# A transformer layer in fp32 on one NeuronCore: PSUM banks of the 16-head attention from one pool of seven by a table, its order and the order of local attention anew

## The chip, the cores and the metric

The kernel runs on one core of one Trainium2 chip. The metric is the device time of one execution in microseconds (us), lower is better. Engines: PE (TensorE, with PEld for its weight loads), DVE (VectorE), ACT (ScalarE), POOL (GpSimd) and SP, which only issues DMAs. Each engine executes its own instruction stream in order; they meet through semaphores.

## What is computed

Eight batches of 512 tokens with 256 channels go through one post-norm layer: self attention with 16 heads of 16 channels, cross attention of the same form against a context of 512 tokens per batch, and then a stack of two layers of local attention (8 heads of 64, windows of 128 keys and the window before) with a gated MLP, seen as 8 x 512 tokens. Everything is fp32; products that need fp32 accuracy are made from two halves of each operand (high and low) in three matmuls.

```python
def _L0_attn_ref(x, w_qkv, w_proj):               # 16 heads, head size 16
    ...
    q = q * cos + _rotate_half(q) * sin
    k = k * cos + _rotate_half(k) * sin
    attn = jax.nn.softmax(jnp.einsum('bhqd,bhkd->bhqk', q, k) * hd ** (-0.5), axis=-1)
    out = jnp.einsum('bhqk,bhkd->bhqd', attn, v)
    return out.transpose(0, 2, 1, 3).reshape(B, N, D) @ w_proj
...
def local_attention(q, k, v):                      # per window of 128 queries: 256 keys
    ...
    sim = jnp.where(mask, -jnp.finfo(sim.dtype).max, jnp.einsum('bhwid,bhwjd->bhwij', bq, bk))
    return jnp.einsum('bhwij,bhwjd->bhwid', jax.nn.softmax(sim, axis=-1), bv)
...
x = _layernorm(x + _L0_attn_ref(x, L0_attn_w_qkv, L0_attn_w_proj), axis=-1)
x = _layernorm(x + _L0_xattn_ref(x, ctx_1024, ctx_1024, ...), axis=-1)
x = _layernorm(x + _L0_ffn_ref(x, ...), axis=-1)
```

## The kernel before, in words

The program is a list of stages, one list for all engines (`all_stages`, L265). A stage is a name with its indices, such as `("rope", vb, qk, tile)`. Each engine walks the whole list and executes its own part of every stage; a part waits on semaphores for what it needs. So the list's order is the order of every queue, SP's and POOL's too, and nothing else sets it.

**16-head part** (`head_stages`, L103; from about 38 to 970 us). It handles 16 "virtual batches" `vb`: 0 to 7 are self attention, 8 to 15 cross attention. A step is one virtual batch and has 16 groups. In a group PE makes four score tiles (`score`, matmul at L594, 128 keys x 512 queries, for `vb`) and four maxima tiles (`amax`, L579, 128 queries x 512 keys, for the virtual batch one step later), always a score beside a maxima tile: a *pair*. The two matmuls of a pair use different halves of the rows. Then `pv` (L610) multiplies the group's four exponentials with V and accumulates in bank 3. For each score tile ACT makes one exp (L829) and for each maxima tile DVE one maximum (L1004). The maxima of a batch, transposed by `maxtr` (L586) and negated, are written into a row of the stacked queries, so scores come out with the maximum taken off.

Between these run the stages that `SELF_ORDER` and `CROSS_ORDER` place. An entry is (place, kind, part, lag): place 0 to 95 in the step, six places for each group, and the stage is done for the virtual batch `step - lag`. Place p lies in group p//6; remainder 0 follows the first pair, 1 and 2 the second, 3 the third, 4 the fourth, and 5 follows pv. So a PE stage at a remainder from 0 to 3 splits the four pairs of a group, and one at 4 or 5 doesn't. PE stages are `tr` (L527, x transposed), `rope` and `bias1` (q and k projections), `val` (v projection) and `proj` (output projection), all through `terms` (L491 to L493), and `maxtr`. Other engines' stages are named for what they make: `mix` and `mix_sum` (rotary), `heads_hi` on ACT (L805) and `heads_lo` on DVE or POOL (L1276), the high and low halves of q and k; `stack` on SP (L1485, 12 DMAs a half in self steps), which places them into QS and KS for `amax` and `score`; `ot`, `ot_out`, `sums`, `inv`, `inv_out`, `spread`, `collect`, `scale`, `out_hi`, `out_lo`: the output, its sums and their reciprocals on the way to `proj`; `res`, `stats`, `rstd`, `norm` (POOL, L1319): residual and layer norm. In step 0 there is nothing to score yet and PE makes maxima alone; in the last step (`LAST_STEP`) scores alone.

**PSUM** has 8 banks of 128 x 512 fp32. `bank_turns` (L276) walks the list once and gives each product its bank: scores go round banks 0 to 2, maxima and all projections and transposes of the 16-head part round banks 4 to 7, pv has bank 3. A PE stage waits until the last user of its bank has been read (`vacant`, L453); the reader's instruction hands it back.

**Local attention** (`window_stages`, L176; two stretches, about 970 to 1360 and 1590 to 1970 us). A unit is one window tile of 128 queries with all 8 heads; there are 32 in each of two layers. `WINDOW_ORDER` is the order of one unit's iteration; an entry is (kind, part, lag), and lags from -2 to 2 let five units overlap. PE stages: `wqk` and `wval` (projections, 6 matmuls each, L491 to L493), `wqkt` (four transposes, L663), `wscore` (L679, four matmuls for two heads), `wpt` (four transposes of probabilities, L688), `wpv` (16 matmuls, L703), `wout` (12 matmuls). The first unit of every four looks at half the keys, so its `wpt` and `wpv` have half the matmuls. POOL makes `wrn`, `wqn` (L1353, L1359: normalized q and k) and `wscale` (L1373, probabilities times reciprocal sums), ACT the exp and most copies from PSUM, DVE the masked maxima and reciprocals. `wswap` (L1464) is ten SP DMAs a unit, which place q and k halves into qT and kT; `wscore` 0 waits for them. Local attention has its banks fixed by kind.

Places of PE's stages in the head part, with a `*` where the place splits a group:

```
self, before:  val 2* 5    tr 7* 8*    rope 12* 18* 18* 27*      maxtr 30* 66*   proj 80* 85*
self, after:   val 7* 91*  tr 7* 8*    rope 14* 21* 31* 39*      maxtr 25* 56*   proj 78* 86*
cross, before: val 3* 6*   tr 13* 14*  bias1 20* 38* 56* 56*     maxtr 25* 66*   proj 81* 87*
cross, after:  val 1* 9*   tr 13* 19*  bias1 25* 38* 51* 55*     maxtr 32* 75*   proj 78* 86*
```

`val` at 91 after the change is for the next virtual batch (lag -1).

Of the kernel before, what the change touches and what calls it, by code (L numbers as in the profile page):

```python
# [23 lines left out]
def f(ap):  # L24
# [13 lines left out]
    (18, "rope_out", (0, 1), -1), (18, "rope_out", (1, 0), -1), (18, "rope", (1, 0), -1), (26, "rope_out", (1, 1), -1), (27, "rope", (1, 1), -1),
    (27, "heads_lo", (0, 1), -1), (29, "ot", (0,), 1), (29, "heads_lo", (1, 0), -1), (30, "negmax", (1,), 1), (30, "maxtr", (1,), 1),
    (31, "norm", (0,), 4), (31, "negmax_out", (1,), 1), (34, "ot_out", (0,), 1), (34, "stats", (1,), 4), (37, "rstd", (1,), 4),  # L40
    (39, "heads_hi", (0, 0), -1), (39, "heads_lo", (1, 1), -1), (40, "out_lo", (1,), 3), (40, "collect", (0,), 2), (40, "scale", (0,), 2),
# [7 lines left out]
CROSS_ORDER = (
    (2, "stack", (1,), 0), (2, "stats", (0,), 4), (3, "val", (0,), 0), (4, "ctx_lo", (0,), -1), (4, "stats", (1,), 4), (4, "ot", (3,), 2),  # L50
    (6, "val_out", (0,), 0), (6, "val_out", (1,), 0), (6, "val", (1,), 0), (8, "collect", (0,), 2), (11, "ctx_lo", (1,), -1), (11, "norm", (1,), 4),
    (12, "tr_hi", (0,), -1), (12, "tr_hi", (1,), -1), (13, "tr_lo", (0,), -1), (13, "tr", (0,), -1), (14, "tr_lo", (1,), -1), (14, "tr", (1,), -1),
    (17, "ot_out", (3,), 2), (18, "sums", (), 2), (20, "bias1_out", (0, 0), -1), (20, "out_hi", (0,), 3), (20, "bias1", (0, 0), -1),
# [211 lines left out]
def all_stages():  # L265
# [1445 lines left out]
```

## Time and profile before

| | |
|---|---|
| median of 3 runs | 2189.59 us (2188.16 to 2189.7) |
| profiled execution | 2188.94 us, its span 2187.2 us |
| mean granted PE clock | 0.982 |
| busy share of the span | PE 96%, PEld 67%, DVE 76%, ACT 69%, POOL 61% |
| 16-head maxima: DVE L1004 | 1024 x 682 ns, 641.4 us |
| 16-head exp: ACT L829 | 1024 x 603 ns, 555.1 us |
| idle of PE ahead of L579 | 17.5 us, 15.8 of it for the DMA of KS |
| chain that ended last | PE 88%, DVE 3%, POOL 3%, SP's queue 2%, ACT 2% |

The span runs from the first to the last instruction; the profiled execution's time holds what lies around it too. Busy time is a union over instructions of one engine. For PE the end of a matmul is modelled, so the start of the next block tells more than the busy share. A row of the timeline has start, duration, engine, line, tiles, how many instructions were joined, and in brackets the idle time before with what ended it. DMA-issuing instructions stand under SPq. The granted clock 1.00 is PE's full speed.

### The profile page before, as it was taken

The numbers are of one execution on the slowest core, as the hardware profiler recorded it, in microseconds if no ns is written. First come the engines' busy times: TensorE is split into PE (matmuls) and PEld (weight loads), VectorE is DVE, ScalarE is ACT, GpSimd is POOL, SyncE is SP. The second block draws the span as 40 slices with busy tenths as digits, with TensorE's granted clock in tenths as the row PEclk, the third lists the DMA queues.
The fourth block names the chain that finished last, engine by engine and source line by source line (L and its number), as shares of the span: only waits on it lengthen the run. The fifth ranks groups of instructions, "written<-read, shape, count | busy, mean of one in ns | idle before, by whom it ended". The sixth has DMA issues, their size and how long they took to land.

```text
span 2187.2 us, 44568 instructions
## 1 busy us (share of the span) xinstructions
PE 2092.9 (96%) x13992; PEld 1472.3 (67%) x13992; DVE 1669.8 (76%) x3989; ACT 1498.5 (69%) x3418; POOL 1330.7 (61%) x1378
## 2 busy tenths in 40 slices
PE   4999999999999999879999999999899999999997
PEld 3544444444444444357888887788778888887887
DVE  5888788888888888558888887565488888875775
ACT  2388788888888888736777777544377777775443
POOL 2444466443445444668888886464378887875775
PEclk8799999999999999989999999999999999999999
DMA  4124333433333333435554544200155555551211
GB/s 131 59 93 128 103 108 109 122 105 111 116 110 115 120 120 115 138 87 148 109 120 107 111 105 115 67 20 6 56 108 114 114 111 108 112 121 44 64 58 44
DMA packets 191072, 216.13 MB, mean 99 GB/s; under 512 B 24128, under 2 KB 117056, under 8 KB 190848
## 3 DMA queue, kind: packets, MB, share of 16 engines
q1 hardware_dynamic: 188288, 204.90, 35.3%
q0 software_dynamic: 2560, 8.39, 1.0%
q8 instruction: 123, 2.02, 0.4%
q14 instruction: 101, 0.83, 0.1%
HBM read 47.14 MB, written 29.89 MB: 35 GB/s over the span
## 4 chain that ended last, share of the span: by engine, by line
PE 88%; DVE 3%; POOL 3%; SPq 2%; ACT 2%; issue 2%; DMA 1%; POOLq 0%; ACTq 0%; DVEq 0%
PE PS L491 15%; PE PS L492 13%; PE PS L493 13%; PE PS L610 11%; PE PS L594 11%; PE PS L579 7%; PE PS L703 5%; PE PS L679 5%; PE PS L688 4%; PE PS L663 2%; SPq L1464 1%; PE PS L586 1%; ACT PT L829 1%; PE PS L527 1%; PE PS L635 1%
## 5 line engine op out<-in xcount | busy, mean ns | idle before, releaser
L1004 DVE TENSOR_REDUCE MX<-PS 128x1 f32<-128x512 f32 x1024 | 641.4, 682 | 145.3 <-PE PS L579 138.1
L829 ACT ACTIVATE PT<-PS 128x512 f32<-128x512 f32 x1024 | 555.1, 603 | 124.1 <-PE PS L594 122.6
L594 PE MATMUL PS<-QS,KS 64*128 64x512 f32 x1024 | 386.4, 455 | 6.1 <-ACT PT L829 5.3
L579 PE MATMUL PS<-KS,QS 64*128 64x512 f32 x1024 | 361.8, 451 | 17.5 <-DMA KS<-HL 15.8
L594 PEld LDWEIGHTS PS<-QS,KS 64*128 64x128 f32 x1024 | 166.2, 185 | 270.2 <-issue 137.0
L1373 POOL TENSOR_TENSOR PB<-PB,RC 128x512 f32<-128x512 f32 (+1 forms) x256 | 250.3, 997 | 48.5 <-DVE RC L1126 48.5
L610 PE MATMUL PS<-PT,VP 128*17 128x512 f32 x2048 | 269.5, 598 | 1.3 <-ACT OT L836 0.6
L890 ACT ACTIVATE PB<-PB,NMf 128x256 f32<-128x256 f32 (+1 forms) x512 | 242.5, 477 | 8.5 <-DVE NMf L1117 8.4
L579 PEld LDWEIGHTS PS<-KS,QS 64*128 64x128 f32 x1024 | 173.1, 189 | 72.8 <-issue 40.9
L1353 POOL TENSOR_TENSOR RI<-RI,mhalf 128x8 f32<-128x8 f32 x128 | 213.3, 1667 | 10.7
L1117 DVE CUSTOM_DVE_ANT_0 PB<-PS,mk 128x256 f32<-128x256 f32 (+1 forms) x512 | 175.7, 385 | 53.7 <-PE PS L679 53.5
L491 PE MATMUL PS<-WQ,XT 128*128 128x512 f32 x384 | 164.3, 428 | 18.4 <-ACT V L872 8.3
L679 PE MATMUL PS<-kT,qT 128*128 128x256 f32 (+1 forms) x1024 | 168.8, 288 | 4.1 <-DMA kT<-kT 2.4
L1297 POOL TENSOR_TENSOR OC<-OC 128x512 f32<-128x512 f32 x32 | 40.9, 1281 | 206.7 <-DMA OC<-od 137.7
L1359 POOL TENSOR_TENSOR RA<-RA,RI 128x512 f32<-128x512 f32 x128 | 133.4, 1042 | 50.5 <-DVE RA L1097 49.9
L866 ACT ACTIVATE SQ<-PS 128x512 f32<-128x512 f32 x128 | 76.5, 598 | 118.9 <-PE PS L493 118.9
L679 PEld LDWEIGHTS PS<-kT,qT 128*128 128x128 f32 x1024 | 146.0, 190 | 16.7 <-issue 2.5
L492 PE MATMUL PS<-WQ,XT 128*128 128x512 f32 x384 | 154.0, 401 | 0.0
L493 PE MATMUL PS<-WQ,XT 128*128 128x512 f32 x384 | 153.8, 400 | 0.0
L902 ACT COPY PTB<-PS 128x512 f32<-128x512 f32 (+1 forms) x256 | 127.9, 525 | 25.4 <-PE PS L688 25.2
L491 PE MATMUL PS<-HT,W 128*128 128x512 f32 x352 | 142.5, 405 | 1.8 <-DVE X L1138 1.0
L493 PE MATMUL PS<-HT,W 128*128 128x512 f32 x352 | 139.3, 396 | 0.0
(186 smaller groups left out, 5158.3 us busy)
## 6 DMA issues: line engine op xcount, KB each, us to landing
qT<-QN SPq DMA_DIRECT2D x384, 128.0 KB
kT<-kT SPq DMA_DIRECT2D x256, 128.0 KB
od<-OT SPq DMA_DIRECT2D x64, 256.0 KB, 2.7
QS<-HL SPq DMA_DIRECT2D x96, 128.0 KB
KS<-HL SPq DMA_DIRECT2D x96, 128.0 KB
QS<-HL SPq DMA_DIRECT2D x48, 256.0 KB
KS<-HL SPq DMA_DIRECT2D x48, 256.0 KB
OC<-od SPq DMA_DIRECT2D x32, 256.0 KB
```

What stands on the lines that cost most here:

```text
L491: pe.matmul(out, L[0], R[0], start=first, stop=False)
L492: pe.matmul(out, L[0], R[1], start=False, stop=False)
L493: return pe.matmul(out, L[1], R[0], start=False, stop=last)
L579: pe.matmul(PS[:, bank, :], QS[rows, s, h // 2, qt * P:(qt + 1) * P], KS[rows, s, h // 2, :], start=True, stop=True).then_inc(fills("amax" ...
L594: pe.matmul(PS[:, bank, :], KS[rows, s, pair, kt * P:(kt + 1) * P], QS[rows, s, pair, :], start=True, stop=True).then_inc(fills("score", v ...
L610: m = pe.matmul(PS[32 * hh:32 * hh + 17, 3, :], VP[:, vb % 2, kt, 4 * g + hh, :], PT[:, kt % 2, hh, :], start=kt == 0, stop=kt == 3)
L679: m = pe.matmul(out[:, h, k0:], qT[:, u % 2, x, h, hp], kT[:, hp, h, keys], start=x == 0, stop=x == 1)
L829: act.activation(PT[:, kt % 2, 2 * i + half], PS[:, TURNS["score", vb, g, kt, half, i][0], :], ACT.Exp).then_inc(drains("score", vb, g, kt ...
L890: m = act.activation(p, p, ACT.Exp, bias=NMf[:, u % 2, hh:hh + 1], scale=-1.0, accum_out=SUM[:, u % 2, hh:hh + 1])
L1004: dve.tensor_reduce(MX[:, vb % 2, h // 8, qt, c:c + 1], PS[:, TURNS["amax", vb, h, qt][0], :], AX, ALU.max).then_inc(drains("amax", vb, h, ...
L1353: pool.tensor_tensor(RI[:, part], RI[:, part], mhalf[:, 0:8], ALU.pow).then_inc(sem["rnorm"], 1)
L1373: pool.tensor_tensor(p, p, RC[:, u % 2, h].unsqueeze(2).broadcast_to([P, 2, 256 - k0]), ALU.mult).then_inc(sem["p_scaled"], 1)
```

## The change

Three edits. `bank_turns` takes the banks of all products of the 16-head part, scores too, from a table `BANKS` of digits out of 0, 1, 2, 4, 5, 6, 7, one for each product in the list's order. `SELF_ORDER` and `CROSS_ORDER` are new, with the same stages. `WINDOW_ORDER` is new, with the same stages (some with another lag). No matmul, reduction, exp or DMA is added or removed.

```diff
 SELF_ORDER = (
-    (1, "out_lo", (0,), 3), (2, "val", (0,), 0), (4, "ot", (3,), 2), (5, "val_out", (0,), 0), (5, "val_out", (1,), 0), (5, "val", (1,), 0),
...
-    (57, "norm", (1,), 4), (57, "maxrows", (1,), 0), (59, "mix", (0, 0), -2), (60, "stack", (0,), -1), (64, "heads_hi", (1, 1), -1),
...
-    (91, "collect", (1,), 2), (93, "mix", (1, 1), -2), (94, "stack", (1,), -1), (94, "mix_sum", (0, 1), -2),
...
+    (54, "inv_out", (), 2), (55, "negmax", (0,), 0), (56, "maxtr", (0,), 0), (59, "heads_lo", (1, 0), -1), (64, "heads_hi", (1, 0), -1),
+    (64, "heads_lo", (1, 1), -1), (65, "ot_out", (1,), 1), (67, "maxrows", (1,), 0), (68, "heads_hi", (1, 1), -1), (72, "scale", (0,), 2),
+    (76, "rstd", (0,), 3), (76, "ot", (2,), 1), (77, "out_lo", (0,), 2), (77, "norm", (0,), 3), (78, "scale", (1,), 2), (78, "proj", (0,), 3),
+    (79, "spread", (), 2), (80, "res", (0,), 3), (85, "ot_out", (2,), 1), (86, "proj", (1,), 3), (88, "mix", (0, 0), -2), (88, "stack", (1,), -1),
+    (89, "res", (1,), 3), (90, "stats", (0,), 3), (91, "val", (0,), -1),
...
 WINDOW_ORDER = (
-    ("wsum", 1, -1), ("wval", None, -1), ("wpt", 0, 1), ("wrot", 1, -1), ("woh", None, 2), ("wpt", 1, 1), ("wout", None, 2), ("wres", None, 2),
-    ("wqk", 0, -2), ("wadd", 1, -1), ("wexp", 2, 1), ("wrn", 0, -2), ("wrecip", 1, 1), ("wv", None, -1), ("wmax", 0, 0), ("wexp", 3, 1),
-    ("wscale", 0, 0), ("wscale", 1, 0), ("wptc", 0, 1), ("wptc", 1, 1), ("wsum", 0, -2), ("wqn", 0, -2), ("chore", None, -1),
-    ("wsq", 0, -2), ("wqkh", 0, -1), ("wswap", (0, 0), -1), ("wscore", 0, 0), ("wqkl", 0, -1), ("wswap", (0, 1), -1), ("wrn", 1, -2), ("wexp", 0, 0), ("wqkt", 0, -1), ("wqkh", 1, -1), ("wswap", (1, 0), -1),
-    ("wptc", 2, 1), ("wmax", 1, 0), ("wqkl", 1, -1), ("wswap", (1, 1), -1), ("wscore", 1, 0), ("wrot", 0, -2), ("wrecip", 0, 0), ("wqkt", 1, -1),
-    ("wexp", 1, 0), ("wptc", 3, 1), ("wadd", 0, -2), ("wpv", 0, 1), ("wpt", 2, 1), ("wmax", 2, 0), ("wpt", 3, 1), ("wqn", 1, -2),
-    ("wscale", 2, 0), ("wscale", 3, 0), ("wsq", 1, -2), ("chore_lo", None, 1), ("wscore", 2, 0), ("wtr", None, -2), ("wtrl", None, -2), ("wtrh", None, -2), ("wmax", 3, 0), ("wol", None, 1), ("wqk", 1, -2), ("wscore", 3, 0), ("wpv", 1, 1),
+    ("wval", None, -1), ("wpt", 0, 1), ("wscale", 2, 1), ("wout", None, 2), ("wqk", 0, -2), ("wscore", 0, 0), ("wqn", 1, -1), ("wqkh", 0, -1),
+    ("wqkt", 0, -1), ("wrecip", 1, 1), ("wswap", (0, 0), -1), ("wres", None, 2), ("wadd", 1, -1), ("wscore", 1, 0), ("wsq", 0, -2), ("wptc", 1, 1),
+    ("wmax", 0, 0), ("wpt", 1, 1), ("wexp", 0, 0), ("wscale", 3, 1), ("wswap", (0, 1), -1), ("wmax", 1, 0), ("wqkl", 0, -1), ("wqkh", 1, -1),
+    ("wptc", 2, 1), ("wptc", 3, 1), ("wswap", (1, 0), -1), ("wpt", 2, 1), ("wswap", (1, 1), -1), ("wsum", 0, -2), ("wmax", 2, 0), ("wqkl", 1, -1),
+    ("chore_lo", None, 0), ("wexp", 1, 0), ("wrot", 0, -2), ("wrn", 0, -2), ("wscore", 2, 0), ("wscale", 0, 0), ("wscale", 1, 0), ("wqn", 0, -2),
+    ("wqkt", 1, -1), ("wscore", 3, 0), ("wpt", 3, 1), ("wrecip", 0, 0), ("wadd", 0, -2), ("woh", None, 1), ("chore", None, -1), ("wol", None, 1),
+    ("wtr", None, -2), ("wtrl", None, -2), ("wtrh", None, -2), ("wsq", 1, -2), ("wpv", 0, 1), ("wexp", 2, 0), ("wv", None, -2), ("wsum", 1, -2),
+    ("wexp", 3, 0), ("wrn", 1, -2), ("wmax", 3, 0), ("wpv", 1, 1), ("wrot", 1, -2), ("wqk", 1, -2), ("wptc", 0, 0),
 )
...
+BANKS = (
+    "01245670124567012456071245607124650712465071245607124560741256074125607412560741256204615472105674201576240517425061742560174206"
...
+)
+
+
 def bank_turns(stages):
 
     turns, n, fills = {}, [0] * 8, [0] * 8
-    ring = [0, 0]
+    banks = iter(BANKS)
 
     def use(key, bank, counted=1):
         n[bank] += 1
@@ -287,12 +311,8 @@
         kind, a = s[0], s[1:]
         if s in (("proj", NV - 1, 0), ("proj", NV - 1, 1)):
             use(s, 3)
-        elif kind in ("tr", "rope", "bias1", "val", "maxtr", "proj", "amax", "fold"):
-            use(s, 4 + ring[0] % 4)
-            ring[0] += 1
-        elif kind == "score":
-            use(s, ring[1] % 3)
-            ring[1] += 1
+        elif kind in ("tr", "rope", "bias1", "val", "maxtr", "proj", "amax", "fold", "score"):
+            use(s, int(next(banks)))
         elif kind == "wtr":
             use(s, 2)
         elif kind == "wqk":
```

## Rows read from the trace of the kernel before

**Rows 1.** Windows of 100 us: busy us (x instructions) by engine, granted clock, DMA share, GB/s.

```profile
core 0: us, PE busy (x) PEld busy (x) DVE busy (x) ACT busy (x) POOL busy (x), PEclk, DMA share, GB/s
500.00:600.00 100.00, 99.85 (x645) 48.62 (x643) 83.90 (x147) 81.64 (x162) 35.93 (x43) 1.00 0.38 124
1100.00:1200.00 100.00, 100.00 (x808) 87.56 (x807) 84.72 (x267) 77.93 (x226) 84.59 (x91) 1.00 0.52 113
```

**Rows 2.** Timeline around 336 us: start, us, engine, line, tiles, [idle before, releaser].

```profile
336.18 0.49 PE L594 MATMUL PS<-QS,KS 64*128 64x512 f32 x1
...
336.75 2.48 DVE L1004 TENSOR_REDUCE MX<-PS 128x1 f32<-128x512 f32 x4 [0.20 <-PE PS L579]
...
337.36 0.18 PEld L594 LDWEIGHTS PS<-QS,KS 64*128 64x128 f32 x1 [0.36 <-ACT PT L829]
...
337.79 1.05 PE L610 MATMUL PS<-PT,VP 128*17 128x512 f32 x8
...
338.77 0.50 PE L594 MATMUL PS<-QS,KS 64*128 64x512 f32 x1
```

**Rows 3.** Timeline of PE, a split group of the same part.

```profile
457.37 0.50 PE L594 MATMUL PS<-QS,KS 64*128 64x512 f32 x1
...
458.04 0.39 PE L491 MATMUL PS<-WO,OCr 128*128 128x256 f32 x1
```

**Rows 4.** Timeline of PE in local attention, one unit, score 0 to score 0.

```profile
1723.13 0.64 PE L679 MATMUL PS<-kT,qT 128*128 128x256 f32 x4
1723.61 0.60 PE L663 MATMUL PS<-ident,RA 128*128 128x128 f32 x4
1723.96 0.73 PE L679 MATMUL PS<-kT,qT 128*128 128x256 f32 x4
1724.52 0.60 PE L663 MATMUL PS<-ident,RA 128*128 128x128 f32 x4
1725.05 1.10 PE L703 MATMUL PS<-PTB,V 128*64 128x128 f32 x16
1726.08 1.09 PE L688 MATMUL PS<-ident,PB 128*128 128x128 f32 x8
1726.92 0.72 PE L679 MATMUL PS<-kT,qT 128*128 128x256 f32 x4
1727.48 0.40 PE L491 MATMUL PS<-WQ,XT 128*128 128x512 f32 x1
...
1728.88 0.65 PE L679 MATMUL PS<-kT,qT 128*128 128x256 f32 x4
1729.45 1.09 PE L703 MATMUL PS<-PTB,V 128*64 128x128 f32 x16
1730.48 0.50 PE L491 MATMUL PS<-WQ,XT 128*128 128x512 f32 x1
...
1731.98 1.03 PE L688 MATMUL PS<-ident,PB 128*128 128x128 f32 x8
1732.77 0.37 PE L491 MATMUL PS<-WOF,OTr 128*128 128x256 f32 x1
...
1735.64 0.56 PE L679 MATMUL PS<-kT,qT 128*128 128x128 f32 x4
```

**Rows 5.** Timelines of ACT and PE in the last step of the 16-head part.

```profile
919.60 2.06 ACT L829 ACTIVATE PT<-PS 128x512 f32<-128x512 f32 x4 [0.53 <-PE PS L594]
920.25 0.50 PE L594 MATMUL PS<-QS,KS 64*128 64x512 f32 x1 [0.46 <-ACT PT L829]
```

**Rows 6.** Waits of DVE from 38 to 98 us: total, times, longest.

```profile
DVE MX L1004 <- PE PS L579: 19.7, 9, 8.0
```

**Rows 7.** Timeline of PE, pv of a first unit (half the keys).

```profile
1700.53 0.66 PE L703 MATMUL PS<-PTB,V 128*64 128x128 f32 x8
```

**Rows 8.** Timeline of SP's queue: the ten swap transfers of a unit.

```profile
1724.85 3.69 SPq L1464 DMA_DIRECT2D qT<-QN  x6
1728.59 2.62 SPq L1464 DMA_DIRECT2D kT<-kT  x4
```

**Rows 9.** Timeline of SP's queue: the last stack transfers of a self step.

```profile
346.25 4.76 SPq L1485 DMA_DIRECT2D KS<-HL  x6
```

More of the change, by code:

```diff
@@ L38 @@
[L38 to L41, printed above, removed]
@@ new lines @@
+    (8, "val_out", (1,), 0), (8, "tr", (1,), -1), (11, "rstd", (1,), 4), (12, "out_hi", (0,), 3), (12, "sums", (), 2), (13, "mix_sum", (0, 1), -1),
+    (14, "rope", (0, 0), -1), (16, "rope_out", (0, 0), -1), (17, "mix", (1, 0), -1), (18, "mix", (1, 1), -1), (19, "rope_out", (0, 1), -1),
+    (19, "collect", (0,), 2), (21, "rope", (0, 1), -1), (23, "mix_sum", (1, 0), -1), (24, "out_hi", (1,), 3), (24, "negmax", (1,), 1),
+    (25, "maxrows", (0,), 0), (25, "maxtr", (1,), 1), (26, "out_lo", (1,), 3), (27, "norm", (1,), 4), (28, "ot", (0,), 1), (29, "ot_out", (0,), 1),
@@ new lines @@
+    (31, "heads_hi", (0, 0), -1), (31, "rope_out", (1, 0), -1), (31, "rope", (1, 0), -1), (33, "negmax_out", (1,), 1), (35, "heads_lo", (0, 0), -1),
+    (39, "collect", (1,), 2), (39, "rope", (1, 1), -1), (40, "mix_sum", (1, 1), -1), (40, "inv", (), 2), (41, "rope_out", (1, 1), -1),
+    (47, "heads_hi", (0, 1), -1), (48, "heads_lo", (0, 1), -1), (49, "negmax_out", (0,), 0), (52, "ot", (1,), 1), (54, "stack", (0,), -1),
+    (54, "inv_out", (), 2), (55, "negmax", (0,), 0), (56, "maxtr", (0,), 0), (59, "heads_lo", (1, 0), -1), (64, "heads_hi", (1, 0), -1),
@@ L48 @@
 )
 CROSS_ORDER = (
[L50 to L53, printed above, removed]
@@ L62 @@
-    (79, "res", (0,), 3), (81, "proj", (0,), 3), (84, "norm", (0,), 3), (87, "proj", (1,), 3), (88, "res", (1,), 3), (91, "load_ctx", (), -2),
+    (1, "stats", (0,), 4), (1, "val", (0,), 0), (3, "ot_out", (3,), 2), (4, "val_out", (0,), 0), (5, "ot", (3,), 2), (6, "stats", (1,), 4),
+    (9, "heads_lo", (0, 0), -1), (9, "val", (1,), 0), (11, "val_out", (1,), 0), (12, "stack", (1,), 0), (13, "tr", (0,), -1), (14, "tr_hi", (0,), -1),
+    (16, "out_hi", (0,), 3), (16, "norm", (0,), 4), (17, "rstd", (1,), 4), (17, "tr_lo", (0,), -1), (17, "maxrows", (0,), 0), (19, "tr_lo", (1,), -1),
@@ new lines @@
+    (19, "tr", (1,), -1), (20, "tr_hi", (1,), -1), (21, "out_hi", (1,), 3), (23, "negmax_out", (1,), 1), (25, "bias1", (0, 0), -1),
+    (25, "bias1_out", (0, 0), -1), (25, "sums", (), 2), (25, "norm", (1,), 4), (29, "ot", (0,), 1), (32, "maxtr", (1,), 1), (32, "ot_out", (0,), 1),
+    (34, "negmax", (1,), 1), (34, "load_ctx", (), -2), (35, "heads_lo", (0, 1), -1), (37, "bias1_out", (0, 1), -1), (37, "heads_lo", (1, 0), -1),
+    (38, "bias1", (0, 1), -1), (39, "ctx_hi", (0,), -1), (42, "ctx_hi", (1,), -1), (42, "scale", (0,), 2), (45, "rstd", (0,), 3),
@@ new lines @@
+    (45, "scale", (1,), 2), (48, "stack", (0,), -1), (48, "heads_hi", (0, 0), -1), (51, "inv_out", (), 2), (51, "bias1", (1, 0), -1),
+    (51, "bias1_out", (1, 0), -1), (52, "inv", (), 2), (52, "ot", (1,), 1), (53, "heads_hi", (0, 1), -1), (54, "heads_hi", (1, 0), -1),
+    (55, "bias1", (1, 1), -1), (58, "add_bo", (), 1), (58, "bias1_out", (1, 1), -1), (59, "out_lo", (0,), 2), (60, "collect", (0,), 2),
+    (63, "heads_hi", (1, 1), -1), (64, "heads_lo", (1, 1), -1), (70, "maxrows", (1,), 0), (72, "ot_out", (1,), 1), (72, "negmax_out", (0,), 0),
@@ L63 @@
+    (75, "maxtr", (0,), 0), (76, "ot", (2,), 1), (78, "proj", (0,), 3), (78, "ot_out", (2,), 1), (78, "negmax", (0,), 0), (80, "ctx_lo", (0,), -2),
+    (82, "res", (0,), 3), (83, "spread", (), 2), (85, "res", (1,), 3), (86, "proj", (1,), 3), (91, "collect", (1,), 2), (93, "ctx_lo", (1,), -2),
+    (94, "out_lo", (1,), 2),
 )
```

34 lines of the change are left out of this document (19 added, 15 removed).

## The prediction, made before the changed kernel ran

> **What bounds the kernel now.** I read first the busy time by stretches [rows 1]. In the 16-head part (100 to 850 us) PE is never idle while DVE and ACT work 80 to 84% of the time; in local attention DVE and POOL reach 85%, PE again 100%. PE's own busy time hides its waits, since the end of a matmul is modelled, so the second view is PE's order of time: I read the distance from the first matmul of a block to the first of the next. Three pictures come out.
>
> In the 16-head part a group is four pairs (one score matmul and one maxima matmul side by side) and then pv. With nothing put in between, the pairs take 1.61 us (336.18 to 337.79) and pv 0.98 [rows 2]. The fourth score starts only after 0.36 us of waiting for ACT's exp, which hands back the bank of the first. With a product put between the second and third pair, two pairs take 0.67 us [rows 3], so both halves 1.33 without a wait. A split group is thus 0.28 us cheaper than a whole one.
>
> In local attention a unit (one window tile) takes 12.51 us from score to score, and its blocks follow without a gap [rows 4]. Here only the number and the order of the blocks count.
>
> At two places the 16-head part is not bound by PE alone. In the last step only scores run: ACT works 2.06 us on four and is idle 0.53 us a group, because the fourth score waits 0.46 us for one of three banks [rows 5]. In the first step only maxima run, and DVE waits nine times, 19.7 us in all; without the first wait of 8.0 (the first transfer) that is 11.7 us [rows 6].
>
> **The change, part by part.** Nothing is added or taken away: every matmul, exp, reduction and DMA stays. What changes is the order on each queue and the bank of each product.
>
> *Pool, whole groups.* A group makes eight products and the pool has seven banks. The first bank back is that of the first score, as now, unless a maxima bank is earlier; PE runs as far as it did. So a whole group stays at 1.61 us. Bounds: no gain, or the whole 0.36 us. I take zero, because the count of banks is the row that is nearest.
> The Trainium skill (Perfetto Trace Analysis, Optimization Strategy) reads the same gap that repeats on the engine that should be saturated as a sign of too little PSUM. By that rule a better use of the banks would shorten it; a rival below prices that.
>
> *Order in steps 1 to 15.* A place p of 96 lies in group p//6; remainders 0 to 3 split it. Self steps go from 9 split groups of 16 to 10, cross steps from 10 to 12. Over all steps, 105 whole groups become 85: 20 x 0.28 = 5.6 us less. Against that, 14 pairs of adjacent projections (places 18 and 56) and 8 pairs of transposes are torn apart. Entering a projection after another kind costs 0.10 us (1.50 for wval after wpv, 1.40 for wqk after scores [rows 4]), and coming back about as much: 22 x 0.2 = 4.4 us more. Eight products come to stand together that did not: 1.6 us less. Sum -3 us, bounds -8 and +4.
> The Trainium skill (TensorEngine Tiling (Array Packing), Key Properties) says that changing the tiling mode drains TensorE, which speaks against this order: every split is two more changes between 64-row and full matmuls. By the rule alone the 20 splits would cost 4 us; the rows show the drain's price inside 1.33, and still less than the wait it replaces.
>
> *Last step.* Scores alone use four banks at once, so with seven the fourth need not wait. A group takes 0.53 + 2.06 = 2.59 us now; without the wait of 0.46 it takes 2.13, still over the 2.06 that ACT works on four [rows 5]. Thirteen groups: 6.0 us. Late next is POOL's chain from one batch's norm to the next batch's output, so I take 5, bounds 0 and 6.
>
> *First step.* val(0) of the first batch moves ahead of the first maxima, into time in which PE waits for the first transfer, and one val of the next batch moves in among the maxima. With seven banks in place of four, DVE has up to six reductions ahead, 6 x 2.48/4 = 3.7 us [rows 2], more than the 1.5 us of a projection. Of the 11.7 us of waiting I take half away, 6 us; bounds -9 and +1, since the next batch's rows also must arrive.
>
> *Local attention.* PE's sequence was: score0, wqkt0, score1, wqkt1, wpv0, wpt2+3, score2, wqk1, score3, wpv1, wval, wpt0+1, wout, wqk0. It becomes: score0, wqkt0, score1, wpt1+2, score2, wqkt1, score3, wpt3, wpv0+1, wqk1, wval, wpt0, wout, wqk0. Block by block from [rows 4] and [rows 7]:
> - wpv: 1.03 + 1.03 now. Eight further matmuls add 0.44 (1.10 for sixteen, 0.66 for eight [rows 4, 7]), so 32 in one block take 1.03 + 0.88 = 1.91. Saved 0.15.
> - wqkt: 0.35 between scores, 0.53 ahead of wpv. Both now stand between scores: 0.18 saved.
> - wpt: 0.84 + 0.79 now; new 0.35 (four, like wqkt) + 0.79 + 0.53 (ahead of wpv) = 1.67: 0.04 lost.
> - scores: 0.48 + 0.56 + 0.56 + 0.57 = 2.17; new 0.48 + 3 x 0.56 = 2.16.
> - projections: wval 1.50 and wqk1 1.40 become one block of twelve: 2.90, nothing saved.
> Sum 0.30 us a unit; 62 of the 64 units lie in the steady part: 19 us. It needs that no other queue becomes late. At 12.2 us a unit POOL goes from 84.6 to 87% and DVE to 87%. POOL's 13% are 1.6 us a unit, which a late exp or reciprocal may use up before PE stands at a wpt; behind a parked POOL wait its own next scaling and the normalized q and k, then wqkt. SP issues ten swap transfers a unit: first at 1724.85, last done at 1731.22, next score0 at 1735.64, so 4.4 us are left for landing [rows 8]. The unit shrinks by 0.3, and by 1.1 more in one unit of four (half the wpt and wpv), so 4.1 or 3.0 are left. I take 3 us for waits in the short units: -16 us, bounds -21 and 0.
>
> The MLP is not touched; in the four passages between phases the order moves DMAs and normalizations by some places: 0, bounds -4 and +4.
>
> **Sum**: -3 - 5 - 6 - 16 = -30 us. The profiled execution took 2188.94 (span 2187.2), so 2158.9; the median of the runs is 0.65 higher: 2159.6, forecast 2160.
>
> **Rivals.**
> A. *Local attention gains nothing*, because the swaps or POOL's scaling take the place of PE as the bound. For: slack falls from 4.4 to 3.0 us in the short unit, and 16 waits of up to 1.4 us are 22 us. Against: even now SP is done early and PE shows no wait for the swaps. Time 2160 + 16 = 2176. Chance 0.13.
> B. *First and last step pay nothing*: there the transfers (stack rows, the sums of the batch before) set the end, and PE and ACT only wait elsewhere. For: both are chains with DMAs. Against: the waits named in the rows are for banks and for PE. Time 2160 + 11 = 2171. Chance 0.12.
> C. *The pool takes the wait out of the whole groups*: 85 x 0.36 = 31 us more, 2129. Against: eight products, seven banks. Chance 0.06.
> D. *Slower: the rows of the next batch land late.* In a self step POOL makes the last lower half of the heads after heads_hi (1, 1), at place 64 before and 68 now; SP parks at stack behind it, with inv_out, ot_out and collect queued behind, and then issues 12 transfers, the last six in 4.76 us to 351.01 [rows 9]. In that step 338.77 is place 66 [rows 2], and at some 0.55 us a place (16 steps in about 850 us) the next step begins near 355: 4 us are left for landing, and four places take 2.2 of them. Once the rows land after the start, PE stands at the first maxima for all of the lateness, in each of seven self steps. For slower by over 0.2% that must be (30 + 4.4)/7 = 4.9 us a step, which is a landing 5 to 9 us later than now. With 6 us a step the time is 2160 + 42 = 2202. For: SP's queue was searched anew and POOL's too. Against: 2.2 us are no 5. Chance 0.08.
> E. *The orders only exchange costs of like size*, within 0.2%: 0.04.
>
> **How the numbers follow.** Forecast 0.57, its own range 2145 to 2166. Faster by over 0.2% (4.4 us, about what a measurement of this kernel can tell from no change) are the forecast, A, B and C: 0.88. The range reaches up to A, 2177, and down to 2145 (all lower bounds of the two surest terms and half of the others); C, D and E, 0.18, are left out.
>
> **What would show it.** Right: score to score 12.2 us in local attention with one block of 32 wpv matmuls of about 1.9 us; whole groups still 1.6 us with the wait for ACT's exp; in the last step no PE wait for a bank and ACT idle under 0.2 us a group; DVE's waits in the first step at half. Wrong: PE waiting for DMA at the first score of a unit, or for POOL at wpt (A); PE waiting for the stack's DMA at the first maxima of a step (D); whole groups at 1.25 us (C).

## The result, and the profile after

The changed kernel takes 2151.72 us (median of 4 runs, 2149.66 to 2152.96) against 2189.57: ratio 0.9828, 95% interval 0.9811 to 0.9845, so 37.9 us less. Forecast were 30 less, 2160, in a range of 2145 to 2177. The profiled execution took 2151.54 us (span 2149.8, mean clock 0.975).

The first question is where the 37.4 us between the two spans lie. For that I read off both traces when PE starts the same matmul: the first maxima tile of a step, the last score, score 0 of a unit.

| PE starts | before | after | gained in the stretch | forecast |
|---|---|---|---|---|
| first maxima of step 0 | 37.24 | 37.07 | 0.2 | |
| first maxima of step 1 | 85.19 | 77.98 | 7.0 | 6 |
| last maxima (end of steps 1 to 15) | 886.83 | 871.09 | 8.5 | 3 |
| last score of the last step | 936.10 | 920.15 | 0.2 | 5 |
| score 0 of unit 0 | 969.72 | 949.89 | 3.9 | 0 |
| score 0 of unit 31 | 1354.33 | 1322.57 | 11.9 | 16 with the next but one |
| score 0 of unit 32 (second layer) | 1588.99 | 1559.32 | -2.1 | 0 |
| score 0 of unit 63 | 1965.42 | 1929.47 | 6.3 | |
| end of the span | 2187.16 | 2149.76 | 1.5 | 0 |

So the total is right within 8 us; in the 16-head part the first step came out as said and the other two terms did not. The windows that answer to [rows 1]:

```profile
core 0: us, PE busy (x) PEld busy (x) DVE busy (x) ACT busy (x) POOL busy (x), PEclk, DMA share, GB/s
500.00:600.00 100.00, 100.00 (x644) 47.15 (x645) 84.38 (x147) 85.29 (x168) 41.88 (x47) 1.00 0.29 102
1100.00:1200.00 100.00, 99.80 (x831) 89.68 (x832) 86.69 (x273) 78.25 (x234) 89.70 (x92) 1.00 0.52 111
```

PE is as full as before; what rose are the others: POOL from 84.6 to 89.7% in local attention, DVE from 84.7 to 86.7%.

The timeline of PE and PEld in a whole group after (it answers to [rows 2]):

```profile
702.97 0.49 PE L614 MATMUL PS<-QS,KS 64*128 64x512 f32 x1
...
704.14 0.18 PEld L614 LDWEIGHTS PS<-QS,KS 64*128 64x128 f32 x1 [0.36 <-ACT PT L849]
...
704.57 0.13 PEld L630 LDWEIGHTS PS<-PT,VP 128*17 128x17 f32 x8 [0.24 <-issue]
```

From 702.97 to 704.57 are 1.60 us, with the same 0.36 of waiting for ACT's exp. Seven banks changed nothing here. Lines are 20 higher than before (L594 is now L614).

A group behind a transpose shows what did change. In the kernel before, two transposes stood together; these are its rows around the pairs that follow them, and then those of the changed kernel, where one transpose stands alone:

```profile
581.55 0.49 PE L579 MATMUL PS<-KS,QS 64*128 64x512 f32 x1
...
581.93 1.29 DVE L974 TENSOR_TENSOR xT<-PS,xT 128x512 fp32r<-128x512 f32 x2 [0.20 <-ACT xT L775]
582.00 0.47 PE L594 MATMUL PS<-QS,KS 64*128 64x512 f32 x1
582.39 1.05 PE L610 MATMUL PS<-PT,VP 128*17 128x512 f32 x8
```

```profile
567.51 0.66 PE L547 MATMUL PS<-ident,X 128*128 128x128 f32 x4
568.10 0.49 PE L599 MATMUL PS<-KS,QS 64*128 64x512 f32 x1
...
568.76 0.62 PE L630 MATMUL PS<-PT,VP 128*17 128x512 f32 x4
```

Two pairs took 0.84 us before (581.55 to 582.39) and take 0.66 now. While DVE (L974) still reads the transposes, they hold two of the four banks of the maxima's rotation. That one transpose stands alone is not the reason: the changed kernel also has six places behind two transposes, and two pairs take 0.66 there too, where the 14 places of the kernel before take 0.83 to 1.00.

Local attention, the unit that answers to [rows 4], timeline of PE:

```profile
1122.35 0.72 PE L699 MATMUL PS<-kT,qT 128*128 128x256 f32 x4 [0.20 <-DMA kT<-kT]
1122.91 0.60 PE L683 MATMUL PS<-ident,RA 128*128 128x128 f32 x4
1123.27 0.72 PE L699 MATMUL PS<-kT,qT 128*128 128x256 f32 x4
1123.83 1.03 PE L708 MATMUL PS<-ident,PB 128*128 128x128 f32 x8
1124.62 0.71 PE L699 MATMUL PS<-kT,qT 128*128 128x256 f32 x4
...
1126.60 1.97 PE L723 MATMUL PS<-PTB,V 128*64 128x128 f32 x32
1128.50 0.49 PE L511 MATMUL PS<-WQ,XT 128*128 128x512 f32 x1
...
1131.38 0.60 PE L708 MATMUL PS<-ident,PB 128*128 128x128 f32 x4
1131.73 0.36 PE L511 MATMUL PS<-WOF,OTr 128*128 128x256 f32 x1
...
1134.62 0.63 PE L699 MATMUL PS<-kT,qT 128*128 128x256 f32 x4
```

12.27 us from score 0 to score 0, 0.24 below the 12.51 of before even with 0.20 of waiting for a late swap; other full units take 12.18 to 12.27. The one block of 32 wpv matmuls takes 1.90 us (1126.60 to 1128.50), the eight transposes between scores 0.79, the twelve projections 2.88.

The last step, timeline of ACT, then of SP's queue:

```profile
898.23 6.05 ACT L849 ACTIVATE PT<-PS 128x512 f32<-128x512 f32 x12
...
906.46 0.62 ACT L860 CAST OCr<-OC 128x512 fp32r<-128x512 f32 x1 [2.18 <-POOL OC L1317]
```

```profile
873.92 2.83 SPq L1570 DMA_DIRECT2D WQ<-f_wqkv  x6
876.80 2.06 SPq L1570 DMA_DIRECT2D WOF<-f_wo  x4
878.91 0.54 SPq L1529 DMA_DIRECT2D od<-OT  x1
885.96 0.57 SPq L1545 DMA_DIRECT2D RT<-od  x1
```

Where nothing else is in the way ACT now makes twelve exps without a gap, 2.0 us a group (PE's pv blocks start at 900.50, 902.46 and 904.42) in place of 2.59 [rows 5]. Then it stands for 2.18 us at POOL's scaling, PE behind it, and the step is no shorter. The same two starts on PE, and the windows of 900 to 925 us (columns as above), with those of the kernel before for 910 to 925 last:

```profile
907.63 0.49 PE L614 MATMUL PS<-QS,KS 64*128 64x512 f32 x1 [1.50 <-ACT PT L849]
...
910.17 1.91 PE L630 MATMUL PS<-PT,VP 128*17 128x512 f32 x8 [2.05 <-ACT OT L856]
912.01 1.22 PE L614 MATMUL PS<-QS,KS 64*128 64x512 f32 x2
```

```profile
900.00:910.00 10.00, 5.89 (x40) 1.57 (x36) 1.01 (x2) 7.82 (x17) 9.48 (x9) 0.94 0.18 68
910.00:925.00 15.00, 13.29 (x71) 6.83 (x72) 7.74 (x22) 7.48 (x15) 9.29 (x13) 0.81 0.21 70
```

```profile
910.00:925.00 15.00, 12.63 (x75) 4.53 (x72) 8.28 (x20) 11.53 (x23) 12.36 (x13) 1.00 0.32 115
```

PE was busy 5.89 of 10 us, and behind that its granted clock falls (a mean of 0.81 over 15 us, that is, part of them at 1.2 GHz in place of 2.4): pv takes 1.84 us (910.17 to 912.01) for 0.98. In the kernel before the same work of the last step stands some 16 us later, and the clock is 1.00 there too (925 to 940 us).

In the first step the waits of DVE, which were 19.7 us before [rows 6], are these (without the first of 8.0 they are 3.0 in place of 11.7):

```profile
DVE MX L1024 <- PE PS L599: 11.0, 7, 8.0
```

### The profile page after: what moved, and what is told of

It is laid out like the page before. It is cut to its first block, busy times and chain, and to the rows that moved or that the text cites. A ratio compares the mean times of both kernels' runs of the same rounds, so it can differ in the third digit from the quotient of the medians.

```text
span 2149.8 us, 44627 instructions
## 1 busy us (share of the span) xinstructions
PE 2060.1 (96%) x13992; PEld 1457.3 (68%) x13992; DVE 1669.9 (78%) x3989; ACT 1483.2 (69%) x3418; POOL 1351.8 (63%) x1378
## 4 chain that ended last, share of the span: by engine, by line
PE 87%; DVE 4%; SPq 2%; ACT 2%; issue 2%; POOL 2%; DMA 1%; POOLq 0%; ACTq 0%; DVEq 0%
PE PS L511 15%; PE PS L512 13%; PE PS L513 13%; PE PS L630 11%; PE PS L614 9%; PE PS L599 7%; PE PS L699 5%; PE PS L723 5%; PE PS L708 4%; PE PS L683 2%; SPq L1484 1%; PE PS L606 1%; DVE MX L1024 1%; PE PS L547 1%; DMA kT<-kT 1%
## 5 line engine op out<-in xcount | busy, mean ns | idle before, releaser
L614 PE MATMUL PS<-QS,KS 64*128 64x512 f32 x1024 | 368.4, 448 | 1.9 <-ACT PT L849 1.5
L599 PE MATMUL PS<-KS,QS 64*128 64x512 f32 x1024 | 355.6, 448 | 8.1 <-DMA KS<-HL 4.9
L614 PEld LDWEIGHTS PS<-QS,KS 64*128 64x128 f32 x1024 | 160.1, 186 | 249.8 <-issue 200.1
L1393 POOL TENSOR_TENSOR PB<-PB,RC 128x512 f32<-128x512 f32 (+1 forms) x256 | 273.3, 1078 | 53.7 <-DVE RC L1146 53.6
L599 PEld LDWEIGHTS PS<-KS,QS 64*128 64x128 f32 x1024 | 164.6, 188 | 70.5 <-issue 52.5
L699 PE MATMUL PS<-kT,qT 128*128 128x256 f32 (+1 forms) x1024 | 175.9, 295 | 10.0 <-DMA kT<-kT 8.6
L511 PE MATMUL PS<-HT,W 128*128 128x512 f32 x352 | 142.4, 404 | 1.5 <-POOL HT L1408 0.8
L708 PE MATMUL PS<-ident,PB 128*128 128x128 f32 x896 | 132.4, 276 | 11.0 <-POOL PB L1393 6.0
L512 PE MATMUL PS<-HT,W 128*128 128x512 f32 x352 | 139.4, 396 | 0.0
L513 PE MATMUL PS<-HT,W 128*128 128x512 f32 x352 | 139.3, 396 | 0.0
```

Source lines behind the costliest of these rows:

```text
L511: pe.matmul(out, L[0], R[0], start=first, stop=False)
L512: pe.matmul(out, L[0], R[1], start=False, stop=False)
L513: return pe.matmul(out, L[1], R[0], start=False, stop=last)
L599: pe.matmul(PS[:, bank, :], QS[rows, s, h // 2, qt * P:(qt + 1) * P], KS[rows, s, h // 2, :], start=True, stop=True).then_inc(fills("amax" ...
L614: pe.matmul(PS[:, bank, :], KS[rows, s, pair, kt * P:(kt + 1) * P], QS[rows, s, pair, :], start=True, stop=True).then_inc(fills("score", v ...
L699: m = pe.matmul(out[:, h, k0:], qT[:, u % 2, x, h, hp], kT[:, hp, h, keys], start=x == 0, stop=x == 1)
```

## The experiments

Twelve kernels. Times are medians of their runs, and differences are taken to the changed kernel's 2151.7 or to the kernel before in the same series (2189.0 to 2190.5). The runs of one kernel spread over 3 to 11 us, so differences of a few us in the medians mean little by themselves. The first four sort the change into its parts.

**Only the order of local attention.** The kernel before, with the new `WINDOW_ORDER`.

> Only the order of local attention is new; the 16-head part keeps its order and its two rotations. Theory A (costs of blocks add up, the parts are independent): local attention saves 18 us as between the two profiles (12 in the first layer, 6 in the second) and the passage into it up to 4, so 2168 to 2172. Rival B (the shorter unit is worth its 18 us only together with the earlier end of the 16-head part, since swaps and normalized q and k start late): 2176 to 2182.

Measured: 2168.0 us, ratio 0.9901 (0.9880 to 0.9922), 21.7 below before. Theory A. The passage from the last score to unit 0's score 0 takes 29.8 us here, 33.6 before and 29.7 in the changed kernel: those 3.9 us are of this order and not of the 16-head part.

**Two pools in place of one, plain rule.** The table's digits are made anew:

```diff
 BANKS = (
-    "01245670124567012456071245607124650712465...
+    scores out of 0 1 2, all else out of 4 5 6 7; the one handed back first in the list's order
```

> All orders are the new ones; but scores may only use banks 0 to 2 and all other products of the 16-head part banks 4 to 7, as before the change (the bank that was handed back first in the list's order). Theory A (the order pays in steps 1 to 15, the pool only in the first and last step, and the last step's gain is lost again): 2153 to 2158, whole groups still 1.60 us. Rival B (the pool is what takes the waits away in steps 1 to 15): 2160 or more, with the excess of 0.18 us behind transposes back.

Measured: 2171.7 us (0.9896 to 0.9937 of before), 20.0 above the changed kernel. Theory A fell, rival B holds: with two pools the new order of the 16-head part is worth nothing (2171.7 against the 2168.0 of the run before, which has the old one).

**One pool, old orders, plain rule.**

> All orders are the old ones; the products of the 16-head part take their bank from one pool of seven, always the one handed back first in the list's order. Theory A: the first step gains some 3 us by deeper work for DVE, the last step's groups go from 2.59 to 2.0 us but the end of the part hardly moves, steps 1 to 15 gain at most the 3 us of the places behind two transposes: 2183 to 2188. Rival B (the pool carries most of the 19 us that the 16-head part gained): 2178 or less.

Measured: 2200.4 us, ratio 1.0050 (1.0036 to 1.0064): slower than before. Neither theory allowed for that. Its timeline behind two transposes shows the price of a badly chosen bank:

```profile
584.41 0.49 PE L612 MATMUL PS<-QS,KS 64*128 64x512 f32 x1
...
585.04 1.80 ACT L847 ACTIVATE PT<-PS 128x512 f32<-128x512 f32 x3
585.71 0.50 PE L612 MATMUL PS<-QS,KS 64*128 64x512 f32 x1 [0.57 <-ACT PT L847]
```

The second score comes 1.30 us after the first, not 0.33. By the list's order its bank was handed back long ago; in time ACT had first to make two casts of the transposes (1.07 us at 584.08), so its exps were late.

**One pool, new orders, plain rule.**

> As the changed kernel, but the table's 2239 digits are made by a plain rule: the bank of the seven that was handed back first in the list's order (only 362 digits agree with the table). Theory A (one pool is enough, which bank does not matter): within 2 us of 2151.7. Rival B (the table was searched and its choice pays): 2155 or more.

Measured: 2165.7 us (0.9865 to 0.9906), 14.0 above the changed kernel with its table. Rival B.

To see the same thing in the traces, I took for each block of one to four pairs from step 1 to the last maxima what it needed beyond the fastest of its kind (0.425, 0.66, 0.89 and 1.60 us). The sums are 11.6 us in the kernel before, 5.3 in the changed one, 19.2 with two pools, 20.2 with one pool and the plain rule, 25.2 with that rule and the old order. The differences account for the length of these steps in the same traces, where the order is the same: 20.2 - 5.3 = 14.9, and the steps took 14.7 us longer; with two pools 19.2 - 5.3 = 13.9 for 13.7, and 6.8 more in the first step. (The whole times differ by 14.0 and 20.0 in the medians, and by some 22 between the profiled executions.) With the plain rule and the new order none of the waits stands directly behind transposes, where the old order under the same rule has 15 of its 25 us; 19 of the 20 us stand in blocks behind a pv. So the pool pays through waits that are not made, and I asked next whether a good choice alone could do it.

The same head part was run in several kernels, which shows how far one trace can be trusted. PE's stretches in all profiled executions, in us:

| 16-head part | traces | step 0 | steps 1 to 15 |
|---|---|---|---|
| old order, two rotations | 3 | 45.8, 45.9, 48.0 | 801.6 to 803.6 |
| old order, one pool, plain rule | 1 | 43.0 | 815.6 |
| old order, one pool, banks by time | 1 | 43.3 | 798.8 |
| new order, two pools, plain rule | 1 | 47.8 | 806.8 |
| new order, two pools, banks by time | 1 | 48.1 | 804.5 |
| new order, one pool, plain rule | 1 | 41.3 | 807.8 |
| new order, the table | 5 | 40.5 to 41.2 | 792.4 to 793.5 |

So the change is worth some 5 to 7 us in step 0 and 8 to 11 in steps 1 to 15, and the profile of the kernel before has the slowest of its three first steps.

**One pool, old orders, banks chosen by time.** For each product a bank that had been handed back by the times of the trace of before.

> All orders are the old ones, with one pool of seven and a table made for them: for each product a bank that, by the times in the trace of the kernel before, was handed back at least 0.15 us before the product starts, the longest free first. Theory A (the pool pays only if no product is given a bank that a transpose, a v projection or a late reader still holds; it then removes the waits that the two rotations had, 5 to 7 of 11.6 us in steps 1 to 15, and those of the first step): 2177 to 2182, so 20 us below the plain rule's 2200.4. Rival B (the old order is what costs, and no table helps it): 2188 or more.

Measured: 2184.3 us (0.9963 to 0.9990), 16.2 below the plain rule and 4.8 below before; the sum of the waits fell from 25.2 to some 8.5 us. Theory A in its direction, 2 us outside its numbers (rival B began at 2188): the old order keeps its whole groups.

**Two pools, new orders, banks chosen by time.**

> The changed kernel's orders, with two pools again (scores in banks 0 to 2, all else in 4 to 7), but the banks chosen well: of its pool always the one that was handed back first by the times in the changed kernel's trace. The run with two pools and the plain rule took 2171.7. Theory A (one pool of seven is needed: two transposes or a v projection hold two of the four banks for over 1 us, and no choice among four avoids the wait): 2165 to 2172. Rival B (the choice of the bank is all, the one pool is not needed): 2151 to 2156.

Measured: 2169.5 us (0.9885 to 0.9919), 18 above the changed kernel. Theory A's range. The choice by time, made from the changed kernel's trace, is worth 2 us with two pools, inside the noise; that no better choice exists was not tried. Where two transposes stand together the two pairs behind them take 1.64 to 1.73 us at all six places, and 0.66 with one pool. Timeline of PE:

```profile
308.53 0.50 PE L599 MATMUL PS<-KS,QS 64*128 64x512 f32 x1
308.53 0.50 PE L614 MATMUL PS<-QS,KS 64*128 64x512 f32 x1
309.65 0.46 PE L599 MATMUL PS<-KS,QS 64*128 64x512 f32 x1 [0.63 <-DVE xT L994]
```

**Only the 16-head part.** The changed kernel with the old `WINDOW_ORDER`.

> The 16-head part is as changed (order and table), local attention keeps its old order. Theory A (parts independent): the new order of local attention alone gave 21.7 us, so what is left of 37.9 is 16: 2172 to 2175. Rival B (the two parts need each other): 2168 or less, or 2178 or more.

Measured: 2173.1 us (0.9908 to 0.9946), 17.4 below before. Theory A; 17.4 + 21.7 = 39.1 for 37.9.

**The last step on three banks.** The digits of the last step's scores become 0, 1, 2 in turn.

> As the changed kernel, but in the last step of the 16-head part, where only scores run, they go round three banks as before. Theory A (that step ends by the chain of sums, reciprocals and scalings of the batch before, which the four-banks-at-once gain of 0.5 us a group only waits for): groups of 2.59 us are back and the time stays at 2151 to 2153. Rival B (the earlier scores are what the passage into local attention gained): 2154 to 2158.

Measured: 2152.1 us (2146.2 to 2153.3). Theory A: the groups of 2.59 us are back, and the fourth bank in the last step is worth nothing. Its trace also shows what became of PE's clock. Window of 910 to 925 us, columns as above:

```profile
910.00:925.00 15.00, 12.49 (x76) 6.05 (x76) 7.75 (x22) 8.77 (x17) 10.79 (x14) 1.00 0.21 71
```

The clock is 1.00 here, and throughout this last step. So it is in all six traces in which the last step's scores use three banks; in all eight in which they use more, 7 to 17 us of it ran at 1.2 GHz. With more banks POOL's scaling starts 33.1 to 34.7 us behind the last maxima in the kernels that leave the weight loads alone, in place of 35.4 to 35.9. From there to the last score are 14.0 to 16.3 us, in place of 13.9 to 14.1. What the chain gained the clock took back, in part or whole.

**The weight loads later.** In `LAST_STEP`:

```diff
-    (32, "spread", (NV - 3,)), (32, "ot_out", (NV - 2, 2)), (32, "load_consts", ()), (32, "load_qkv", (0, None)),
+    (32, "spread", (NV - 3,)), (32, "ot_out", (NV - 2, 2)), (32, "load_consts", ()),
...
-    (35, "collect", (NV - 2, 0)), (35, "collect", (NV - 2, 1)),
+    (35, "collect", (NV - 2, 0)), (35, "collect", (NV - 2, 1)), (35, "load_qkv", (0, None)),
```

> The changed kernel, with the ten weight loads for local attention issued by SP behind the last step's ot_out, sums and collect in place of ahead of them. Theory A (the last step gave nothing because od<-OT is issued 5 us late behind these loads and then lands after 7.0 us in place of 2.8, and the sums, the reciprocals and the layer norm hang on it): od lands 5 to 9 us earlier, the last scores come 4 to 8 us earlier: 2143 to 2148. Rival B (the last step is set by POOL's layer norms and the rotation tables on DVE, which come when they come): 2150 to 2153; or the loads then arrive late for the splits and local attention starts late: 2154 or more.

Measured: 2156.1 us (2148.8 to 2160.2; 0.9836 to 0.9876 of before), no gain; the median lies in the last of rival B's ranges, 2154 or more. The first half of theory A is right and didn't help: the last score comes 51.0 us behind the last maxima, not 49.1. SP's queue in its timeline:

```profile
877.87 0.33 SPq L1529 DMA_DIRECT2D od<-OT  x1
879.93 0.56 SPq L1545 DMA_DIRECT2D RT<-od  x1
889.46 1.81 SPq L1537 DMA_DIRECT2D OC<-od  x2
891.36 2.78 SPq L1570 DMA_DIRECT2D WQ<-f_wqkv  x6
894.19 2.30 SPq L1570 DMA_DIRECT2D WOF<-f_wo  x4
896.53 0.57 SPq L1522 DMA_DIRECT2D QS<-NM  x1
```

RT is issued 2.06 us behind od, no longer 7.05. But SP then parks at collect (L1537) for POOL, which frees OC after its layer norms, and my edit had put the loads behind that wait and ahead of the negated maxima (QS<-NM), which now go out at 896.53 in place of 890.36. A second chain, POOL's, is as long as the first.

**And the rotation tables earlier.** As above, with `rot` ahead of `inv`.

> As the run with late weight loads, and DVE makes the rotation tables (3.6 us) ahead of the reciprocals of the last step, in time in which it waits for a transfer. Theory A (these 3.6 us stand in the chain once the transfer is early): 2 to 4 us below that run. Rival B (another wait in the last step covers them): within 1 us of it.

Measured: 2151.6 us (2151.4 to 2154.4), 4.5 below the run before it in the median, outside both theories. But its last score comes later (924.05 against 923.01 in the profiled runs), and that run's own times spread over 11 us; whether the tables stood in the chain stays open. Against the changed kernel neither edit gains.

**pv in halves.** 79 of the 84 whole groups that the trace has in steps 1 to 15; the matmuls of pv are split by columns:

```diff
-                    m = pe.matmul(PS[32 * hh:32 * hh + 17, 3, :], VP[:, vb % 2, kt, 4 * g + hh, :], PT[:, kt % 2, hh, :],
+                    m = pe.matmul(PS[32 * hh:32 * hh + 17, 3, cols], VP[:, vb % 2, kt, 4 * g + hh, :], PT[:, kt % 2, hh, cols],
```

> The changed kernel, with pv of the group before made in two halves of 256 columns in 79 of the whole groups, the first between the second and third pair, the second where pv stood. Theory A (a whole group costs 1.60 us only because the fourth score waits for the exp of the first; anything put between the pairs takes that wait away): a group saves 0.28 us of waiting and pays 0.11 us for one more entry into pv, 79 times, at most 13 us, and DVE at 2.48 us for four maxima may keep half of that: 2139 to 2147. Rival B (half a pv costs nearly as much as a whole one, or DVE and ACT set the pace at once): 2152 or more.

Measured: 2151.5 us (2149.3 to 2153.2): nothing, and half a us short of rival B's 2152. Its timeline says why (PE, with one row of DVE):

```profile
647.55 0.49 PE L617 MATMUL PS<-QS,KS 64*128 64x512 f32 x1
...
648.21 0.63 PE L634 MATMUL PS<-PT,VP 128*17 128x256 f32 x8
648.76 0.50 PE L602 MATMUL PS<-KS,QS 64*128 64x512 f32 x1
...
649.43 0.63 PE L634 MATMUL PS<-PT,VP 128*17 128x256 f32 x8
649.99 0.50 PE L617 MATMUL PS<-QS,KS 64*128 64x512 f32 x1
...
651.08 0.63 PE L634 MATMUL PS<-PT,VP 128*17 128x256 f32 x8 [0.36 <-ACT PT L854]
```

```profile
648.11 3.73 DVE L1029 TENSOR_REDUCE MX<-PS 128x1 f32<-128x512 f32 x6 [0.39 <-PE PS L602]
```

The split group takes 2.44 us (647.55 to 649.99) and not 2.59, with no wait for the exp: the mechanism of theory A is right, and half a pv costs 0.56 against 0.98 for the whole, so 0.13 for the split. But in the next group two pairs take 1.09 (649.99 to 651.08), not 0.66. The wait that the trace names there, 0.36 us, is for ACT's exp; ACT had a rotary cast (L830) between two exps. DVE needs 2.5 us for four maxima, a little more than the split group, and works without a gap too. Over steps 1 to 15 the account closes: 79 groups at 1.32 in place of 1.60 give 22 us back, pv costs 10.6 more, and what the blocks of pairs take beyond their fastest grows by 12, to some 17. Of these 17, by the releasers that the trace names, some 7.5 are waits for ACT's exp and 1.4 for DVE's maxima; for most of the rest it names none. ACT and DVE are both busy 83 to 84% of that time, and which of the two sets the pace stays open.

**wpv together, all else as before.**

```diff
-    ("wexp", 1, 0), ("wptc", 3, 1), ("wadd", 0, -2), ("wpv", 0, 1), ("wpt", 2, 1), ("wmax", 2, 0), ("wpt", 3, 1), ("wqn", 1, -2),
+    ("wexp", 1, 0), ("wptc", 3, 1), ("wadd", 0, -2), ("wpt", 2, 1), ("wmax", 2, 0), ("wpt", 3, 1), ("wqn", 1, -2),
...
-    ..., ("wscore", 3, 0), ("wpv", 1, 1),
+    ..., ("wscore", 3, 0), ("wpv", 0, 1), ("wpv", 1, 1),
```

> The kernel before, with one edit in local attention: the first wpv block stands directly ahead of the second. Theory A (PE's blocks set the unit, and a block costs what it costs beside its neighbours): wpv 2.05 to 1.90 us, wqkt ahead of wpt 0.35 in place of 0.53 and wpt 0.79 in place of 0.85, so 0.39 us a full unit and 22 us in all: 2165 to 2170. Rival B (wpt 2 and 3 then come 1.0 us earlier than now and wait for POOL's scaling, or the copies behind them come late): 2175 to 2190.

Measured: 2226.7 us, ratio 1.0175 (1.0153 to 1.0196), 36.1 slower than before, worse than rival B's 2175 to 2190. From its timeline, PE and POOL:

```profile
1734.16 2.04 POOL L1373 TENSOR_TENSOR PB<-PB,RC 128x512 f32<-128x512 f32 x2
...
1735.26 0.66 PE L688 MATMUL PS<-ident,PB 128*128 128x128 f32 x4
```

```profile
1736.25 0.66 PE L688 MATMUL PS<-ident,PB 128*128 128x128 f32 x4 [0.34 <-POOL PB L1373]
1736.67 0.72 PE L679 MATMUL PS<-kT,qT 128*128 128x256 f32 x4
```

The first wpt starts when POOL's first scaling is done (half of the 2.04 us from 1734.16), the second when its second is: from 1735.26 to 1736.67 are 1.41 us where the two transposes need 0.79. The unit takes 13.13 us (1733.18 to 1746.31), 0.62 more than before, though wpv itself fell to 1.90. The first wpv of before was the cover under which POOL scaled.

## Why the prediction was right, and where only in sum

**Local attention: right in its blocks and its sum.** Forecast 0.30 us a full unit and 16 in all; measured 18.2 between the profiles (11.9 + 6.3), 21.7 with the passages in a kernel of its own. The gain is not even over the units: from score 0 to score 0 four units in a row took 12.27, 11.81, 12.51 and 12.50 us and take 12.23, 11.13, 12.25 and 12.21, so 0.04, 0.68, 0.26 and 0.29, a mean of 0.32. The forecast counted the blocks of the unit of 12.51 alone. wpv 1.90 (said: 1.91), wqkt 0.36 both times, wpt between scores 0.79. Of the 3 us set aside for late swaps in short units most came: PE waits for them 0.20 us in the first layer (unit 14, the wait shown) and 0.33, 0.52 and 1.50 in the second (units 46, 58 and 62), 2.6 in all. (The kernel before waits for swaps too, 2.4 us, but for other units: 4, 30, 31 and 63.) The three of the second layer recur in most traces of the new order. So rival A was near: SP's last swap of unit 14 is issued by 1120.03, 2.3 us ahead of score 0, where the forecast left 3.0. And the run with wpv together is the rival's other half, POOL's scaling, come true: the block sum alone forecasts 2168 for it, and it took 2227.

**First step: right.** 7.0 us for 6 (5 to 7 over all traces), and DVE's waits at a quarter. It is the pool's: with two pools the step takes as long as before, with one pool in the old order 43.0 to 43.3 us of the 45.8 to 48.0, and the new order takes some 2 more away only together with the pool.

**Steps 1 to 15: the gain was larger and of another kind.** The forecast took the pool at zero for whole groups, and that held (1.60 us, 0.36 of waiting; rival C did not come). The 20 fewer whole groups and the torn pairs came out as said: the q and k projections take 88.5 us in 56 blocks where they took 85.6 in 42, the transposes 15.4 in 22 where they took 14.3 in 14, 4.0 us more for the 4.4 of the forecast. The step that failed is the one before: "both halves 1.33 without a wait" was taken from one undisturbed place, and the 11.6 us by which blocks of pairs exceeded their fastest elsewhere (some 13 in the other two traces of this head part) were left out of the account. 6.3 of them went, 3.0 behind the transposes of x and 2.0 behind those of the maxima. The change has one pool and a table for that, and neither would do alone: the new order with two pools gains nothing, the pool with a plain rule and the old order loses 11, with a good table it gains 5; together 17. I had costed the table at nothing by looking only at the whole group; the places to look were those where some banks are held for longer, first of all the pairs behind a transpose, where two banks are held until DVE has read them.

The Trainium skill (Perfetto Trace Analysis, Optimization Strategy) says that consistent bubbles can mean too little buffer space. At the bubble that I held against it, the whole group, the runs agree with the row: seven banks leave it at 0.36, and with pv in halves the time comes back as other waits. At the bubbles that I had not looked at, behind transposes, this case agrees with the page: 0.84 us became 0.66, and 1.64 or more with two pools.

**Last step: wrong.** The 5 us were read from the wait for a bank [rows 5], which is real and is gone. But it covered a chain of the same length: od<-OT, which carries the sums, is issued behind ten weight loads and lands 7.0 us later, reciprocals, `res`, POOL's two layer norms and its scaling follow, and ACT and PE stand until that is there. POOL's scaling began 34.0 us behind the last maxima for 35.4, and from there to the last score are 15.0 us for 13.9. PE pays for the slack with its clock: 0.86 us on the pv shown, 1.1 on the projection behind it (2.75 us from its first matmul to the next score, where 1.62 is the rule). The forecast named POOL's chain as late next and charged it 1 us of 6; the chain and the clock took all. The step that failed is this price, and the term for the clock that was not there. The run on three banks shows that the banks are worth nothing there, the one with late loads that a second chain (POOL, then collect) is as long as the first. Rival B was right for the last step and wrong for the first.

**Passages: the 3.9 us** that the last step missed came between the last score and unit 0, from the new order of local attention, which starts its first units from another point. Forecast was 0, bounds -4 and +4. That the sum still came within 8 us is in part luck: 5.5 us more in steps 1 to 15 and 3.9 in this passage stand against 4.8 less in the last step and 2.1 lost between the layers.

**Rival D** did not come: SP's stack of the next batch ends at 342.57 and the step begins at 345.83, 3.3 us for landing where it was 3.8. The slack shrank by 0.5 us, not by the 2.2 that the rival took from the places.

## What to carry to other kernels

Cost a bank allocation at the products that hold their bank longest, not at the most frequent group: which bank a product gets was worth 14 to 16 us here, and a rule that goes by the order of the program in place of the time of handing back made the same pool, with the old order, slower than two fixed rotations. Before a wait is booked as a gain, ask what is late next at the same place: three waits that were really taken away (the last step's bank, the transfer behind the weight loads, the exp of the whole group) gave nothing, since other waits stood close behind each: POOL's chain and the clock, SP parked at POOL, ACT and DVE. And a block that looks like mere work may be another engine's cover: moving 16 matmuls by one place cost 0.6 us a unit.

## What the runs showed of the hardware that I had not expected

Shortening the scores of the last step made PE idle in one stretch (5.89 of 10 us busy), and the next 15 us ran at a mean clock of 0.81 where the kernel before, and the changed kernel with three banks there, had 1.00. All fourteen traces divide this way: no low clock in the last step with three banks, 7 to 17 us of it with more. A faster stretch that ends in a wait can so slow the work behind it. The forecast had no term for the clock in the last step.

The transfer od<-OT of this step lands 2.0 us after its issue in both kernels that issue the ten weight loads later, and 5.0 to 7.0 us after it in the twelve that issue them just ahead of it (7.05 to the issue of its successor in the changed kernel). What holds it up behind them no run separates. Splitting eight pv matmuls of 512 columns into twice eight of 256 costs 0.13 us a time (0.56 + 0.56 - 0.98). Whether that is the entry into the block or the eight further instructions this run can't tell; two blocks of wpv made one, with the same 32 matmuls, saved 0.16 (2.06 to 1.90), which speaks for the entry.
